# Norm sums on the accumulator output of the scalar engine, three mixing products in one block, the fourth beside the fifth, centring ahead of the third

## The reference, cut to what matters

```python
xa = _ln(x, ln1_w, ln1_b)
sx = jnp.concatenate([state[:, 1:2] - xa[:, :1], xa[:, :-1] - xa[:, 1:]], axis=1)
xxx = jnp.tanh((xa + sx * maa_x) @ maa_w1).reshape(b, l, 5, DM)
xxx = jnp.einsum('blfd,fde->blfe', xxx, maa_w2)
xm = xa[:, :, None] + sx[:, :, None] * (maa_stack + xxx)
xk, xw, xv, xr, xg = (xm[:, :, j] for j in range(5))
w = jnp.exp(-jnp.exp(time_decay + jnp.tanh(xw @ td_w1) @ td_w2)).reshape(b, l, h, s_)
r, k, v = xr @ Wr.T, xk @ Wk.T, xv @ Wv.T
g = jax.nn.silu(xg @ Wg.T)
# scan over time: a = k v^T; out = r (u * a + s); s = a + w * s
og = (out - mean) / sqrt(var + 1e-05) per head, * gn_w + gn_b
x1 = x + og * g @ Wo.T
xc = _ln(x1, ln2_w, ln2_b)          # then the channel mix
rr = jax.nn.sigmoid(xr2 @ Wfr.T)
kk = jnp.square(jax.nn.relu(xk2 @ Wfk.T))
return x1 + rr * (kk @ Wfv.T)
```

## Time and profile before

| | us |
|---|---|
| three timed runs | 1116.63, 1121.56, 1121.56 |
| median | 1121.56 |
| the profiled execution | 1118.86 |
| its span in the profile | 1117.1 |

### The profile page before, as it was taken

The page is one execution under the profiler, slowest core; times in us unless marked ns, Lnnn a source line. Parts: engine busy times, 40 slices in busy tenths (PEclk is TensorE's granted clock), DMA queues, the critical chain, the costliest instruction groups (busy, mean ns, idle before and its releaser), DMA issues.

```text
span 1117.1 us, 34410 instructions
## 1 busy us (share of the span) xinstructions
PE 1061.3 (95%) x12992; PEld 883.5 (79%) x12992; DVE 916.1 (82%) x1662; ACT 702.6 (63%) x1606; POOL 608.1 (54%) x535
## 2 busy tenths in 40 slices
PE   5999999999999998999999999999999998788898
PEld 4888988888889887777787877777777776566687
DVE  5997777888777776228999999999999999999753
ACT  5678878777777775465556555456555455544574
POOL 4787887877887885024443454443454443444233
PEclk9999999999999998999999999999999999998999
DMA  8500000011111110013333331233331233304011
GB/s 328 174 4 2 0 0 2 3 41 41 41 48 38 38 47 3 1 28 68 79 83 86 85 70 40 64 81 84 84 76 40 56 82 86 85 10 114 20 38 57
DMA packets 39867, 65.01 MB, mean 58 GB/s; under 512 B 4384, under 2 KB 26208, under 8 KB 39392
## 3 DMA queue, kind: packets, MB, share of 16 engines
q1 hardware_dynamic: 39776, 63.75, 21.4%
HBM read 55.35 MB, written 8.39 MB: 57 GB/s over the span
## 4 chain that ended last, share of the span: by engine, by line
PE 60%; DVE 27%; issue 7%; ACT 3%; DVEq 1%; DMA 1%; SPq 0%; POOL 0%; ACTq 0%; POOLq 0%
PE psum L353 9%; DVE shared L1788 9%; PE psum L267 5%; PE psum L999 5%; PE psum L336 5%; PE psum L1008 4%; PE psum L368 4%; PE psum L1089 4%; DVE shared L1774 4%; PE psum L297 4%; PE psum L280 3%; DVE late_mixed L1754 3%; PE psum L1270 2%; PE psum L310 2%; PE psum L1300 2%
## 5 line engine op out<-in xcount | busy, mean ns | idle before, releaser
L1788 DVE TENSOR_TENSOR_SCAN shared<-late_wT,shared 128x512 f32<-128x512 f32 x128 | 192.4, 1503 | 0.0
L232 POOL TENSOR_TENSOR shared<-shared,att_row_max 128x512 f32<-128x512 f32 x128 | 132.3, 1051 | 17.9 <-DVE att_row_max L564 17.9
L353 PE MATMUL psum<-shared 128*128 128x128 f32 x1024 | 126.6, 277 | 0.0
L453 ACT ACTIVATE shared<-shared 128x512 f32<-128x512 f32 x128 | 80.5, 631 | 67.7 <-POOL shared L232 67.6
L353 PEld LDWEIGHTS psum<-shared 128*128 128x128 f32 x1024 | 121.0, 194 | 0.3 <-ACT shared L462 0.2
L999 PE MATMUL psum<-late_glnT,w 128*128 128x256 f32 x512 | 119.5, 387 | 1.8 <-ACT late_glnT L1378 1.8
L1008 PE MATMUL psum<-w,late_hT 128*128 128x256 f32 x512 | 120.0, 383 | 1.0 <-ACT late_hT L1387 0.9
L564 DVE TENSOR_REDUCE att_row_max<-shared 128x8 f32<-128x512 f32 x128 | 86.9, 680 | 40.9 <-POOL shared L225 40.9
L903 POOL TENSOR_TENSOR shared<-shared,late_rT 128x512 f32<-128x512 f32 x32 | 40.7, 1273 | 140.6 <-DVE shared L1788 140.6
L894 POOL TENSOR_TENSOR late_xm<-late_mixed,late_xa 128x512 f32<-128x512 f32 x64 | 79.7, 1255 | 59.9 <-DVE late_mixed L1754 56.3
L999 PEld LDWEIGHTS psum<-late_glnT,w 128*128 128x128 f32 x512 | 95.8, 192 | 17.9 <-issue 2.8
(11 more groups left out here) (168 smaller groups left out, 2420.9 us busy)
## 6 DMA issues: line engine op xcount, KB each, us to landing
shared<-v_rows SPq DMA_DIRECT2D x64, 512.0 KB, 7.1
shared<-in_enc SPq DMA_DIRECT2D x64, 128.0 KB, 2.6
v_rows<-shared SPq DMA_DIRECT2D x64, 64.0 KB, 1.8
out<-x SPq DMA_DIRECT2D x16, 256.0 KB, 2.0
x<-in_x SPq DMA_DIRECT2D x7, 512.0 KB, 9.7
w<-in_w SPq DMA_DIRECT2D x2, 1024.0 KB, 16.9
shared<-in_cross_mask SPq DMA_DIRECT2D x1, 1024.0 KB, 11.4
shared<-in_w_qkv SPq DMA_DIRECT2D x1, 768.0 KB, 4.5
```

Source lines behind the costliest of these rows:

```text
L232: nc.gpsimd.tensor_tensor(zs, zs, peak.unsqueeze(2).to_broadcast([P, PAIRS, S]), ALU.subtract).then_inc(shifted, 1)
L353: last = nc.tensor.matmul(dst[:, half * P:(half + 1) * P], w[:, kb, c0 + half * P:c0 + (half + 1) * P], src[:, u % 2, kb, 0:P], start=(kb ...
L453: nc.scalar.activation(probs[:, u % 2, half * 4:(half + 1) * 4, :].rearrange("p r k -> p (r k)"), z[:, u % 2, half, :], ACT.Exp).then_inc( ...
L1788: nc.vector.tensor_tensor_scan(states, wT[:, u, half, :, :, :].rearrange("p j b t -> p (j b t)"), states, 0.0, ALU.mult, ALU.add).then_inc ...
```

## The change

1. **Sums on ACT.** `mlp_moments` leaves DVE (bn_stats, bn_aggr and a scaling) for ACT: a copy of each tile into the scratch tile `xn` with the sum as accumulator output, two small scalings, then a square with the shifted mean as bias and the sum as accumulator output. It stands between the second and the third gelu pair. `make_stats` becomes `out_means` (ahead of `square`) and `out_variances` (ahead of the first table load of the body), on ACT too; after the last body both stand in a row at three places. `ch_variances` goes.
2. **Three mixing products at once.** `mix_three` makes the first three, into `even`, `odd` and `o_bank`, where `mix_pair` 0 stood. It waits also for `o_copied`. The second `mix_pair` goes.
3. **The fourth beside the fifth.** `mix_two` makes both where `mix_last` stood, the fifth now from 32 of the rows, the fourth into `proj`; it waits for the copy of NV.
4. **Order on DVE.** `centre` and `mix` 2 come at n = 3, `mix` 3 at n = 5.

```diff
+        ch_mean, ch_var = core.stats[:, 0:TILES], core.stats[:, TILES:2 * TILES]
+        mix_banks = (even, odd, o_bank, proj)
...
+            def mix_three(r):
+                pe.wait_ge(mixer_tanh, r + 1)
...
+                if later(r):
+                    pe.wait_ge(bonus_v_ready, r)
+                if later(r - 1):
+                    pe.wait_ge(o_copied, r - 1)
+                if later(r - 2):
+                    pe.wait_ge(x_ready, r - 2)
+                for half in range(HALVES):
+                    for k in range(3):
...
+                        last = nc.tensor.matmul(mix_banks[k][:, half * RT:(half + 1) * RT],
...
+            def mix_two(r):
+                pe.wait_ge(mixed_ready, r * NMIX + 2)
+                pe.wait_ge(copied, r * 3 + NV)
+                fourth = slice(MIX[3] * DM, (MIX[3] + 1) * DM)
                 for half in range(HALVES):
                     for c, bank in enumerate((even, odd)):
...
+                        rows = slice(c * DD, c * DD + DM)
+                        nc.tensor.matmul(bank[:, half * P:(half + 1) * P], core.maa_w2b[rows, c, half * P:(half + 1) * P],
+                                         mixer_b[rows, :], start=True, stop=True)
+                    last = nc.tensor.matmul(proj[:, half * RT:(half + 1) * RT],
+                                            core.maa_w2a[fourth, half * P:(half + 1) * P], mixer_a[fourth, :],
+                                            start=True, stop=True)
+                last.then_inc(mix_ready, 2)
...
                 elif m == NG:
                     pe.wait_ge(copied, r * 3 + NV)
+                    pe.wait_ge(mixed_ready, r * NMIX + 4)
...
+                if q == 0 and there(r + 1):
+                    pe.wait_ge(mixed_ready, (r + 1) * NMIX + 3)
...
                 if mixing:
-                    mix_pair(s + 1, 0)
+                    mix_three(s + 1)
...
                 if mixing:
-                    mix_pair(s + 1, 2)
                     project(s + 1, NW)
...
-                    mix_last(s + 1)
+                    mix_two(s + 1)
...
+            def mlp_moments(g):
+                act.wait_ge(mlp_x, g + 1)
+                if later(g):
+                    act.wait_ge(xnT_ready, g)
+                act.nop(nofuse=True)
+                for c in range(CH):
+                    last = nc.scalar.activation(xn[:, c, :], core.x[:, ds(g * CH + c, C)], ACT.Copy,
+                                                accum_out=mlp_sum[:, c:c + 1])
+                last.then_inc(mlp_sum_ready, 1)
+                act.wait_ge(mlp_sum_ready, g + 1)
+                nc.scalar.activation(mlp_shift[:, :], mlp_sum[:, :], ACT.Copy, scale=-(C ** -1.5)).then_inc(mlp_mean_ready, 1)
+                nc.scalar.activation(neg_mean[:, :], mlp_sum[:, :], ACT.Copy, scale=-1.0 / C).then_inc(mlp_mean_ready, 1)
+                act.wait_ge(mlp_mean_ready, 2 * g + 2)
+                act.nop(nofuse=True)
+                for c in range(CH):
+                    last = nc.scalar.activation(xn[:, c, :], core.x[:, ds(g * CH + c, C)], ACT.Square, scale=C ** -0.5,
+                                                bias=mlp_shift[:, c:c + 1], accum_out=moments[:, CH + c:CH + c + 1])
+                last.then_inc(moments_ready, 1)
...
+            def out_means(r):
...
+                    last = nc.scalar.activation(xn[:, c, :], core.x[:, ds(t, C)], ACT.Copy, accum_out=ch_mean[:, ds(t, 1)])
...
+            def out_variances(r):
...
+                    nc.scalar.activation(xn[:, c, :], core.x[:, ds(t, C)], ACT.Square, scale=C ** -0.5,
+                                         bias=out_shift[:, c:c + 1], accum_out=ch_var[:, ds(t, 1)]).then_inc(stats_ready, 1)
...
-                    for q in range(UPS):
-                        gelu(s + 3, q)
+                    gelu(s + 3, 0)
+                    gelu(s + 3, 1)
+                if there(s + 2):
+                    mlp_moments(s + 2)
+                if there(s + 3):
+                    gelu(s + 3, 2)
+                    gelu(s + 3, 3)
...
+            make_stats(RUNS - 3)
             square(RUNS - 1)
...
             ch_tanh(EARLY + 3, 1)
+            make_stats(RUNS - 2)
             channel(EARLY + 3, 1)
             ch_copy_in(EARLY + 6, 0)
+            make_stats(RUNS - 1)
             nc.scalar.preload_act_table_set("natural_log_exp_and_others")
...
-                    if n == 4:
+                    if n == 3:
                         if there(s - 1) and not s_is(s, RUNS - 1):
                             centre(s - 1, 1 - u)
                         if there(s + 1):
                             mix(s + 1, 2)
-                            mix(s + 1, 3)
+                    if n == 4:
                         if early(s):
                             ch_mix(early_run(s, 1), 1)
                     if n == 5:
+                        if there(s + 1):
+                            mix(s + 1, 3)
```

More of the change, by code:

```diff
@@ L1594, in body @@
                     ch_tanh(early_run(s, 0), 0)
+                if there(s - 2) and not s_is(s, RUNS - 1):
+                    out_means(s - 2)
                 if there(s - 1) and not s_is(s, RUNS - 1):
@@ L1606, in body @@
                         set_states(s + 1, 1)
+                if there(s - 2) and not s_is(s, RUNS - 1):
+                    out_variances(s - 2)
                 if not s_is(s, RUNS - 1):
@@ L1945, in body @@
                             ch_mix(early_run(s, 0), 0)
-                        if there(s + 2) and not s_is(s, -2):
-                            mlp_moments(s + 2)
                         if there(s - 2) and not early(s):
@@ L1952, in body @@
                         mix(s + 1, 1)
-                    if n == 3 and there(s - 2) and not s_is(s, RUNS - 1):
-                        make_stats(s - 2)
-                    if s_is(s, RUNS - 4) and n == 4:
-                        ch_variances(0)
-                    if n == 4:
+                    if n == 3:
                         if there(s - 1) and not s_is(s, RUNS - 1):
@@ L1981, in _ @@
             attention_residual(1, end)
-            mlp_moments(0)
             spreads(att.first_mlp)
@@ L2006, in _ @@
             add_residual(RUNS - 1)
-            make_stats(RUNS - 1)
-            ch_variances(2)
             ch_mix(EARLY + 5, 1)
```

101 lines of the change are left out of this document (32 added, 69 removed).

## The result

| kernel | median, us | profiled execution, us | its span, us |
|---|---|---|---|
| before | 1119.36 (13 runs) | 1118.86 | 1117.1 |
| changed | 1125.92 (13 runs) | 1124.31 | 1122.5 |

The change makes the kernel slower by half a percent: ratio 1.005, with a 95% interval of 1.0039 to 1.0060. Medians are 6.6 us apart, spans 5.4. The prediction had 1127.0, in a range of 1118 to 1135.

A forecast was written before the change was run, and what follows sets the result against it. DVE was taken to set the steady body, PE only 0.17 us shorter. Terms 3.6 + 1.6 + 1.0 - 0.9 - 1.7 - 0.7 + 1.3 + 2.6 gave +6.8: 1125.7 profiled, 1128.4 by median; 1127 taken, range 1118 to 1135.

The forecast's parts named there:

- to the gate of run 14: After body 15: DVE loses 1.54 us, 1.3 counting; run 13's sums on ACT add 2.6; net +1.3.
- Which full engine waits: Steady body: DVE sets it, PE's stream is 0.17 us shorter; PE additions beyond that show in full.
- (a): PE, mix_three: 12 short passes for 8 on row tiles side by side, block stays at 1.06 us; 0.
- (b): PE before NW: the removed 1.06 us block had covered the last gelu; 0.91 wait laid bare, gain only 0.08.
- (c): PE, mix_last becomes mix_two: 0.65 us becomes 1.06 as two wide products join; +0.41.
- (d): PE, decay's block: switch from 32-row to 64-row tiles after mix_two adds 0.2 us to its 0.45.
- worth at most that: Steady body: whatever is taken off DVE gains at most PE's 0.17 us wait at NR.
- What is queued behind the new waits: Waits of mix_three and mix_two cost 0; DVE's third product has 0.3 us slack before NR.
- 1 (a cheap `mix_two` and switch): Rival at L1059 and L1101: (c) + (d) cost 0.3 us for 0.61; time 1120 to 1123; chance 0.21.
- 2 (a true gain of the block): Rival before NW: NW need not wait, bodies -1 to 11 gain 0.91 more each; about 1115; chance 0.11.
- 3 (a dear accumulator output): Rival on ACT: at 0.40 us per output, PE stands 0.5 longer in 13 bodies; 1135; chance 0.11.
- 4 (DVE's slack at NR): Rival: the 0.3 us slack is missing as POOL holds up scans; 0.5 a body, 1132; chance 0.05.

The follow-up runs named there:

- run 0: No follow-up kernel: the first run inside each kernel, numbered from 0; its MLP residual starts at 462.08 us in the changed kernel.
- run 15: No follow-up kernel: the last run inside each kernel (RUNS - 1); its sums on ACT took 2.28 us on the changed kernel's final chain.
- three experiments that fill it: Changed kernel with other PE work ahead of NW: both head-sum blocks (1123.79 us), the MLP down-projection's first quarter (1122.58), or half that quarter (1115.05).
- the sums alone: Kernel before with only the norm sums moved to ACT, mixing products as before: 1114.82 us, ratio 0.9966 to the kernel before.
- the changed order alone: Changed kernel with PE's head sums behind ch_receptances and NV in bodies 13 and 14 only: 1123.70 us, ratio 1.0045 to the kernel before.
- the mixing part alone: Kernel before with the change's mixing products and DVE order, sums staying on DVE: 1125.86 us, ratio 1.0055 to the kernel before.
- run 13: No follow-up kernel: a run inside each kernel (RUNS - 3); its sums on ACT took 2.38 us on the changed kernel's final chain.
- two relatives of the changed kernel: Changed kernel with the down-projection's first quarter ahead of NW (1122.58 us), and with head sums behind ch_receptances and NV in bodies 13 and 14 (1123.70).

## Why the prediction was right, and where its terms were off

By term, in us of the two profiled executions (5.4 between their spans):

| term | predicted | measured |
|---|---|---|
| start of the MLP residual of run 0 (not the change's) | 0 | +0.53 |
| body -2 | +1.0 | +0.30 |
| bodies -1 to 1 | +1.6 | +1.73 |
| bodies 2 to 11 | +3.6 | +3.11 |
| body 12 | -0.9 | -0.88 |
| body 13 | -1.7 | -1.03 |
| body 14 | -0.7 | +0.15 |
| to the gate of run 14 | +1.3 | -0.79 |
| the sums of run 15 | +2.6 | +2.31 |

- **Which full engine waits.** Right. Taking DVE's 1.94 us away is worth 0.27 a steady body by itself, and putting them back costs nothing once PE is the bound.
- **(a)** 1.07 for 1.06. **(b)** The gap before NW is 0.93 for 0.91, which was taken from the prologue (1.02 in the bodies outside the hardware loop). This was the step that decided: three experiments that fill it gain 0.46, -0.06 and 0.68 a body, by what else they lay bare, and none gives more than the gap. **(c)** 1.07 for 1.06. **(d)** 0.65 for 0.65, and a cause of its own. The sum of the four was +0.53; bodies -1 to 1 show 0.58 each. In bodies 2 to 11, 0.31 each for 0.36: the wait that went was 0.27 with the sums alone and not 0.17. So "worth at most that" was too low. The 0.17 was read in one early body, where the average over bodies 6 to 11 is 0.28.
- **ACT.** The moments took 2.4 for 2.9, since an accumulator output takes only 0.09 us until the next instruction starts. That is also most of the 0.3 by which run 15's sums came out cheaper, and of body -2.
- **Bodies 13 and 14: the step that failed.** "What is queued behind the new waits" goes through `mix_three`, `mix_two` and the third product, and leaves out the fourth wait in the diff: the head sums wait for DVE's third mixing step. I also had only steady bodies in mind. In bodies 13 and 14, `ch_receptances`, NV, `mix_two` and `decay` stand behind those sums, with `ch_values` last, and DVE waits for that. I had -2.4 for the two, it was -0.9, and the changed order alone took 2.7 off. With it the bodies are 2.25 and 1.36 shorter than before, so my -1.7 and -0.7 were also too small for what leaving DVE is worth. The 1.96 and 1.95 of the mixing part alone are no price of that wait: 1.6 us of each is PE at the lower clock.
- **To the gate of run 14.** 0.9 of the difference is a granted clock that stood lower in the first execution of before and not in the second. Against the second the term is +0.13 for +1.3. Taking the sums of run 13 off the chain gave 1.89, so DVE's side had given about 1.89 - 0.13 = 1.8 where I let 1.3 count, and the sums cost about 1.9 where I had 2.6. Each of these two kernels still has one fall in this stretch, and in two relatives of the changed kernel such a fall goes with 0.32 us (49.83 for 49.51), so both figures are good to a few tenths.
- **The total** comes near by some luck, because the errors have both signs: bodies 13 and 14 +1.5 over my terms and the start +0.5, this stretch -2.1, body -2 -0.7, bodies 2 to 11 -0.5, the end -0.3. The medians differ by 6.6, the forecast for the profiled execution was +6.8.
- **Rivals.** 1 (a cheap `mix_two` and switch) is out by 1.07 and 0.65. 2 (a true gain of the block) is out by the gap. 3 (a dear accumulator output) is out: 0.2 each, 0.09 effective. 4 (DVE's slack at NR) did not show with the change; it shows at 0.2 once PE's gap is filled, and its cause then is ACT.

## What to carry to other kernels

When a block goes from the bounding engine, look at what its two neighbours wait for: its length is the gain only if the neighbour's input was ready long before. Where two engines hand each other work several times in a loop, one block of cover is needed for each hand-over, and a large one can be split (here two halves of 0.87 us for gaps of 0.93 and 0.77). Price a new wait in every kind of body the code runs in, the last two as well: list each added wait of the diff, and for each the queue behind it. Before a stretch of one profile is compared with the same stretch of another, compare the granted clock in it.

## What the runs showed of the hardware

- An accumulator output on ACT is an instruction of its own, ACTIVATION_READ_ACCUMULATOR, of 0.18 to 0.20 us, but the next instruction starts 0.09 us after it began: from 684.94 to 685.34 the copy with its output takes 0.40 as a step.
- A change of the rows of PE's tiles from 32 to 64 costs the next block 0.20 us (0.45 to 0.65), measured with nothing else changed in that block.
- TensorE's granted clock falls to its lower level (1.2 GHz) after gaps of PE's work in the tail, yet not each time. The same block of eight passes (L1270) at the same place took 2.88 us in one execution of the same kernel and 2.01 in the other; PE had been idle 2.90 us ahead of it in the one and 2.89 in the other; only in the first was the lower level granted during the block. With mixing alone a fall on the chain of body 13 cost 1.6 us; the one near 990 us cost nothing, in a body where DVE is the bound. So a difference of one or two us in bodies 13, 14 or the tail between two single profiles says nothing about a change until the clock is compared.

```profile
1053.27 2.88 PE psum L1270 x8
```

```profile
1052.09 2.01 PE psum L1270 x8
```
